# First attention: the maximum and the exponential of wide score tiles in two pieces

## The reference

```python
scores = jnp.einsum('bqd,bkd->bqk', Qr, Kr) / jnp.sqrt(jnp.float32(d))
mask = jnp.tril(jnp.ones((T, T), dtype=bool), k=1)
scores = jnp.where(mask[None, :, :], scores, -jnp.inf)
attn = jax.nn.softmax(scores, axis=-1)
out = jnp.einsum('bqk,bkd->bqd', attn, V)
```

## Time and profile before

| | before |
|---|---|
| median of 3 runs | 703.73 us |
| lowest to highest | 703.64 to 704.94 us |
| profiled execution | 704.66 us |
| its span | 702.9 us |
| granted TensorE clock | 0.994 |
| TensorE busy in the span | 634.1 us, 90% |
| VectorE busy | 528.9 us, 75% |
| ScalarE busy | 489.2 us, 70% |
| GpSimd busy | 188.3 us, 27% |

### The profile page before, as it was taken

How to read it: one execution, slowest core, us unless ns; L and a number is a source line. 1 busy time by engine, 2 the same in 40 slices (tenths; PEclk the granted TensorE clock), 3 DMA queues, 4 the chain that set the end, 5 groups by cost and what they waited for, 6 DMA issues and landing times.

```text
span 702.9 us, 9405 instructions
## 1 busy us (share of the span) xinstructions
PE 634.1 (90%) x3324; PEld 272.4 (39%) x3324; DVE 528.9 (75%) x993; ACT 489.2 (70%) x503; POOL 188.3 (27%) x250
## 2 busy tenths in 40 slices
PE   7989899999999899889988888898898788899996
PEld 4677345464464423223222112122231111266555
DVE  6876512427155399999899999999999999676775
ACT  4656324225333499999999999999999989444431
POOL 4532240212102041491148101705600006022012
PEclk9999999999999999999999999999999989999999
DMA  5430200002204301234013510111102103300171
GB/s 171 134 137 1 92 1 0 2 0 59 77 1 137 111 11 47 57 105 138 5 57 97 151 56 11 49 57 56 31 27 57 56 3 120 119 1 1 41 232 30
DMA packets 33230, 44.60 MB, mean 63 GB/s; under 512 B 5408, under 2 KB 20000, under 8 KB 32800
## 3 DMA queue, kind: packets, MB, share of 16 engines
q1 hardware_dynamic: 33184, 44.01, 21.1%
HBM read 31.60 MB, written 10.55 MB: 60 GB/s over the span
## 4 chain that ended last, share of the span: by engine, by line
PE 43%; ACT 23%; DVE 21%; issue 11%; POOL 1%; DVEq 0%; ACTq 0%
ACT w_hh L1138 19%; PE ps L778 8%; PE ps L788 8%; DVE hid L1482 5%; DVE hid L1477 5%; PE ps L813 5%; PE ps L760 4%; PE ps L690 3%; PE ps L671 3%; PE ps L744 2%; PE ps L822 2%; ACT probs L1109 2%; DVE st L1240 2%; PE ps L587 1%; PE ps L493 1%
## 5 line engine op out<-in xcount | busy, mean ns | idle before, releaser
L1138 ACT ACTIVATE w_hh<-hid 128x2048 f32<-128x2048 f32 x128 | 249.9, 1952 | 8.3 <-DVE hid L1482 7.8
L690 PE MATMUL ps<-w_hh,v_h 128*32 128x512 f32 x1024 | 137.8, 610 | 33.4 <-ACT w_hh L1138 32.3
L1477 DVE TENSOR_TENSOR hid<-ps,probs 128x1024 f32<-128x1024 f32 x86 | 104.5, 1215 | 19.4 <-ACT probs L1109 16.1
L671 PE MATMUL ps<-q_s,k_s 64*128 64x512 bf16 x256 | 99.3, 389 | 14.7 <-DVE hid L1477 14.1
L1482 DVE SCALAR_TENSOR_TENSOR hid<-ps,probs 128x1024 f32<-128x1024 f32 x86 | 104.7, 1217 | 4.6 <-PE ps L671 3.3
L671 PE MATMUL ps<-q_w,k_w 64*128 64x512 bf16 x256 | 99.4, 389 | 0.0
L1109 ACT ACTIVATE probs<-ps 128x1024 f32<-128x1024 f32 x86 | 91.3, 1062 | 2.2 <-PE ps L671 2.2
L671 PE MATMUL ps<-q_g,k_s 128*128 128x512 bf16 x256 | 78.3, 388 | 1.1 <-ACT qkv_a L1109 1.1
L671 PEld LDWEIGHTS ps<-q_w,k_w 64*128 64x128 bf16 x256 | 23.7, 92 | 107.2 <-issue 55.3
L788 PE MATMUL ps<-hid,w_hh 128*128 128x512 f32 x128 | 56.3, 592 | 0.0
L778 PE MATMUL ps<-hid,w_hh 128*128 128x512 f32 x128 | 55.8, 594 | 0.0
(11 more groups left out here) (314 smaller groups left out, 1001.2 us busy)
## 6 DMA issues: line engine op xcount, KB each, us to landing
qk_rows<-part SPq DMA_DIRECT2D x48, 128.0 KB, 2.4
w_hh<-w_rows SPq DMA_DIRECT2D x4, 1024.0 KB, 8.8
qk_rows<-part_g SPq DMA_DIRECT2D x24, 128.0 KB, 2.4
q_g<-qk_rows SPq DMA_DIRECT2D x32, 96.0 KB, 2.2
k_s<-qk_rows SPq DMA_DIRECT2D x32, 96.0 KB, 2.3
q_s<-qk_rows SPq DMA_DIRECT2D x32, 96.0 KB, 2.4
k_w<-qk_rows SPq DMA_DIRECT2D x32, 96.0 KB, 2.5
q_w<-qk_rows SPq DMA_DIRECT2D x32, 96.0 KB, 2.4
```

Source lines behind the costliest of these rows:

```text
L671: last = mm(ps[:, base + half, :], k_op[rows, u, keys], q_op[rows, u, half * CHUNK:(half + 1) * CHUNK], start=True, stop=True)
L690: last = mm(ps[VW * g4:VW * g4 + VW, 6, :], v_h[:, u, mt, :], ee[:, mt % 2, g4 * CHUNK:(g4 + 1) * CHUNK], start=(mt == 0), stop=(mt == BT ...
L1138: A(ee[:, mt % 2, :], zz[:, mt % 2, :], ACT.Exp).then_inc(S["e"], 1)
L1477: v.tensor_tensor(zz[:, mt % 2, 0:SEQ], banks[:, 2 * CHUNK:4 * CHUNK], gg[s % 3], ALU.add).then_inc(S["z1"], 1)
```

## The change

For tiles with i >= 4 the maximum and the exponential are each made in two pieces, columns 0 to 511 and the rest; tiles with i < 4 keep one piece. `a_scores` counts `s_a` after each bank, so the first maximum waits for the first bank alone. `nmx` is now made from both maxima, the second one read as an operand per row. Each exponential has a sum of its own, `rsum` and `rsum_1`, and `a_next` adds them before the reciprocal. `a_turn` waits for the first exponential before its first four transposes and for the second before the fifth. The counts of `e_a` and `s_a` are kept by `pieces_to`. The order of the tiles and of the other work on each engine stays as it was.

```diff
--- before.py
+++ after.py
@@ -204,6 +204,7 @@
         sm = sb("sm", [P, SM_W])
         tiny = sb("tiny", [P, 64])
         nlam = sb("nlam", [P, 1])
+        mx_1, rsum_1 = tiny[:, 0:TILES], tiny[:, TILES:2 * TILES]
         cs_tab = sb("cs_tab", [P, 2, CT, HEADS, 2])
         raw = sb("raw", [P, 2, CHUNK])
         sq = sb("sq", [P, 2, CHUNK])
@@ -325,6 +326,13 @@
             if b == 0 and i < 2:
                 return 1
             return 2 * b + (2 if P * (i + 1) < CHUNK else 3)
+
+        def pieces(t):
+
+            return 2 if t % BT >= CT else 1
+
+        def pieces_to(t):
+            return sum(pieces(u) for u in range(t + 1))
 
         def att_width(i):
 
@@ -548,7 +556,7 @@
                 pe.wait_ge(S["ropeq"], seen)
                 pe.wait_ge(S["ropek"], seen)
                 if t >= 2:
-                    pe.wait_ge(S["e_a"], t - 1)
+                    pe.wait_ge(S["e_a"], pieces_to(t - 2))
                 w = att_width(i)
                 for n0 in range(0, w, CHUNK):
                     n1 = min(w, n0 + CHUNK)
@@ -560,17 +568,21 @@
                     if masked:
                         last = mm(ps[:, bank, m0 - n0:m1 - n0], ident_bf[:],
                                   mask[:, m0 - P * i:m1 - P * i], start=False, stop=True)
+                    if n0 == 0 and pieces(t) == 2:
+                        last.then_inc(S["s_a"], 1)
                 last.then_inc(S["s_a"], 1)
 
             def a_turn(t):
                 i = t % BT
-                pe.wait_ge(S["e_a"], t + 1)
+                pe.wait_ge(S["e_a"], pieces_to(t) - pieces(t) + 1)
                 if t == 0:
                     pe.wait_ge(S["vout"], 2)
                 if t == 4:
                     pe.wait_ge(S["vout"], CHUNKS)
                 pe.wait_ge(S["pe_a"], t)
                 for j in range(i + 1):
+                    if j == CT:
+                        pe.wait_ge(S["e_a"], pieces_to(t))
                     last = nc.tensor.transpose(ps[:, 4 + j // CT, (j % CT) * P:(j % CT + 1) * P],
                                                probs[:, t % 2, j * P:(j + 1) * P], ident[:])
                 last.then_inc(S["pt_a"], 1)
@@ -989,8 +1001,10 @@
                 if t >= 2:
                     act.wait_ge(S["pt_a"], t - 1)
                 base = 2 * CHUNK * (t % 2)
-                A(probs[:, t % 2, 0:w], banks[:, base:base + w], ACT.Exp, bias=nmx[:, t:t + 1],
-                  scale=ATT_SCALE, accum_out=rsum[:, t:t + 1]).then_inc(S["e_a"], 1)
+                for i, total in enumerate((rsum, rsum_1)[0:pieces(t)]):
+                    n0, n1 = i * CHUNK, w if i == pieces(t) - 1 else CHUNK
+                    A(probs[:, t % 2, n0:n1], banks[:, base + n0:base + n1], ACT.Exp, bias=nmx[:, t:t + 1],
+                      scale=ATT_SCALE, accum_out=total[:, t:t + 1]).then_inc(S["e_a"], 1)
 
             def a_turned(t):
                 i = t % BT
@@ -1317,10 +1331,18 @@
 
             def a_max(t):
                 w = att_width(t % BT)
-                dve.wait_ge(S["s_a"], t + 1)
                 base = 2 * CHUNK * (t % 2)
-                me.step(v.tensor_reduce(mx[:, t:t + 1], banks[:, base:base + w], AX.X, ALU.max))
-                v.tensor_scalar(nmx[:, t:t + 1], mx[:, t:t + 1], -ATT_SCALE, None, ALU.mult).then_inc(S["m_a"], 1)
+                if pieces(t) == 2:
+                    dve.wait_ge(S["s_a"], pieces_to(t) - 1)
+                    me.mark(v.tensor_reduce(mx_1[:, t:t + 1], banks[:, base:base + CHUNK], AX.X, ALU.max))
+                n0 = CHUNK * (pieces(t) - 1)
+                dve.wait_ge(S["s_a"], pieces_to(t))
+                me.step(v.tensor_reduce(mx[:, t:t + 1], banks[:, base + n0:base + w], AX.X, ALU.max))
+                if pieces(t) == 2:
+                    v.tensor_scalar(nmx[:, t:t + 1], mx[:, t:t + 1], mx_1[:, t:t + 1], -ATT_SCALE,
+                                    ALU.max, ALU.mult).then_inc(S["m_a"], 1)
+                else:
+                    v.tensor_scalar(nmx[:, t:t + 1], mx[:, t:t + 1], -ATT_SCALE, None, ALU.mult).then_inc(S["m_a"], 1)
 
             def a_add(c):
                 dve.wait_ge(S["yn_a"], c + 1)
@@ -1328,10 +1350,12 @@
 
             def a_next(t):
 
-                dve.wait_ge(S["e_a"], t + 1)
+                dve.wait_ge(S["e_a"], pieces_to(t))
                 w = P * (t % BT + 1)
                 if t % BT < BT - 1:
                     me.mark(v.tensor_copy(p_next[:, t:t + 1], probs[:, t % 2, w:w + 1]))
+                if pieces(t) == 2:
+                    me.step(v.tensor_tensor(rsum[:, t:t + 1], rsum[:, t:t + 1], rsum_1[:, t:t + 1], ALU.add))
                 me.step(v.reciprocal(rinv[:, t:t + 1], rsum[:, t:t + 1]))
 
             def a_post(t):
```

## The result

| | before | after |
|---|---|---|
| median of 8 runs | 703.93 us | 706.50 us |
| lowest to highest | 703.43 to 704.98 | 705.85 to 708.75 |
| profiled execution | 704.66 us | 707.50 us |
| its span | 702.9 us | 705.7 us |

The ratio after to before is 1.0040, 95% interval 1.0027 to 1.0054: slower by 1.9 to 3.8 us. The forecast had the sign right and the size wrong: 705.3 us, +1.57, against +2.6 between the medians. (The forecast added to a median of 703.73 us from three executions; the median of eight is 703.93.)

A forecast was written before the change was run, and what follows sets the result against it. VectorE was taken to bound the kernel up to tile 7, then TensorE with ScalarE close behind, VectorE again before tile 15. Terms 1.03 + 0.54 = +1.57 us on a median of 703.73 gave 705.3 us; range 704.1 to 706.4.

The forecast's parts named there:

- The bound: First attention: VectorE's order of work sets exponential starts up to tile 7 (41.06 us); then TensorE, with ScalarE close behind.
- Part 1, second maximum: Maximum of each wide tile on VectorE: the second piece adds 0.08 us (bounds 0.06 and 0.16), earning nothing.
- part 2, pointer: `nmx` of each wide tile, reading the second maximum through a pointer: +0.07 us (bounds 0 and 0.10).
- Part 3, the addition: Adding the two sums on VectorE between copy and reciprocal: 0.17 us each (bounds 0.13 and 0.22).
- rival B: Expensive operations at tiles 7 and 15: no overlap (0.16), addition 0.22, pointer 0.10; 2.3 us, 706.0 us; chance 0.17.
- Part 4 and the sum: Two-piece exponential: ScalarE free 0.24 us later, transposes end 0.23 sooner; all terms: 1.03 (batch one) + 0.54 (tile 15) = +1.57.
- The slack of 0.15 us: ScalarE's margin before TensorE loads tile 8's transpose; subtracted from the 1.18 us shift, leaving 1.03.
- The two rules weighed beside the rows: Skill rules: next operation waits for an empty pipe (sum 1.97, 705.7 us); small tiles pay fixed latency (0.158 and 0.244).
- C: Hand-over by halves works: each wide tile's chain 0.6 us shorter, 4.9 us on eight tiles; 698.8 us; chance 0.05.
- A: Same mechanism, cheap operations at tiles 7 and 15: pointer free, addition 0.13; 1.1 us, 704.8 us; chance 0.28.
- its rider: Addition to rival B: `nmx` of tile 5 or 6 also stands behind GpSimd (0.93 us); 706.6 us.
- D: Pieces start no earlier and VectorE's additions are absorbed by stalls; only ScalarE's 0.24 us stays; 704.0 us; chance 0.05.

The follow-up runs named there:

- e1: The changed kernel with the addition of the two sums written as a tensor_scalar through a pointer; stage +1.61 us against the kernel before, ratio 1.0021.
- e4: The changed kernel with the exponential in one piece again (no second sum, no addition), maximum in two; stage +0.73 us against the kernel before, ratio 1.0010.
- e6: The kernel before with GpSimd's four rotary additions cut from 512 columns to 8 each; stage -0.98 us against the kernel before, ratio 0.9981.
- e2: The kernel before plus one 128x1 tensor_tensor ahead of the reciprocal of each wide tile; stage +1.62 us against the kernel before, ratio 1.0022.

## Why the prediction was wrong

*The bound.* Right. VectorE set the time up to tile 7, and every 0.1 us put on it there appeared in the stage (e1 to e4). TensorE is close behind, though: with GpSimd's additions cut it sets part of the time (e6), which the prediction did not say.

*Part 1, second maximum, and part 2, pointer.* Right. The pieces start 0.61 us apart, 0.08 short of the first one's 0.69, and `nmx` took 0.214 us instead of 0.153. All eight second maxima start 0.60 to 0.61 us after the first. Priced 0.15 a tile; taking the split of the maximum away gave 0.66 for five tiles, 0.13 each.

*Part 3, the addition.* This step failed. I took 0.17 us, between a step of another stage (0.15) and the step behind the reciprocal of tile 4 (0.18), and gave 0.22 as the upper bound. At tile 4 it took 1.17 us, 1.0 more than priced, and it lay on the path: without it (e1) the stage is 0.86 us shorter, although the addition through the pointer takes 0.05 us more than the free one each time. The signs were in front of me. I had used the post-scaling held up by GpSimd and let only `nmx` stand behind GpSimd as an addition to rival B, for 0.6 us. I did not ask the same of the addition, although it runs at 36.2 us, while GpSimd works until 37.4, and although the rows that I used show no `tensor_tensor` on two SBUF tensors beside GpSimd. I also halved the merged row of GpSimd's two operations and so read the post-scaling as ending 0.3 us behind the first; that one ends at 36.16 (34.50 + 1.66), and the scaling 0.08 us later, at 36.24: it waits for the end of the first and the addition for the end of the second. A bound from below or above has to come from a row in the same neighbourhood, not only of the same size. The Trainium skill says it too ("SBUF — State Buffer", section "SBUF: two separate sides"): a VectorE instruction in a mode with two ports, or one with two SBUF inputs when the GpSimd instruction reads SBUF, and the GpSimd instruction exclude each other; whichever starts first keeps the other out until it is done. The runs agree (1.17 to 1.19 us until GpSimd's end, three kinds; GpSimd's 1.66 instead of 1.27 behind VectorE), and I had not weighed it.

*Part 4 and the sum.* Right. Without the hold-up, the exponential of tile 7 in e1 was 0.97 us late against tile 4's maximum (0.94 forecast), the stage +1.61 (1.57). The way through ScalarE's norm behind tile 7 and tile 15 was as forecast: from tile 7 to tile 11 the shift in the changed kernel grew from 1.89 to 1.98 us, which is 0.24 - 0.15, and the tail added 0.49 (0.54 forecast; 0.55 in e1). The transposes of tile 15 ended 2.15 us after the start of the exponential (2.12 forecast) instead of 2.35, and that was useless, as said.

*The slack of 0.15 us.* I took it off the whole shift. It belongs only to the way through ScalarE; e2 and e4, with one-piece exponentials, kept the whole shift of tile 7.

*The two rules weighed beside the rows.* The Trainium skill's section "The DRAIN you can't avoid" ("VectorE: DVE Perf Modes") adds that a next operation that is not held starts earlier; the prediction left that out. Here the second maxima start 0.08 us before the end of the first, so the extra 0.4 us of that paragraph did not come. The section on the errata speaks of operations that read SBUF, while the 0.158 and 0.244 us are from operations that read PSUM: these rows do not bear it out.

*The rivals.* C (the hand-over by halves, 0.05) did not come: one wide maximum in eight would have waited for scores, and the changed kernel has no wait for TensorE ahead of a wide maximum. A and B had the right mechanism at other prices. B's sum of 2.3 us comes near the measured 2.47, and its rider's 706.6 near the median of 706.5, but by luck: operations do overlap, and what is held up is the addition, while all eight `nmx` took 0.21 us. D did not hold.

*The range* ended at 706.4, the median was 706.5; that this is so near is due to B's terms in the range, not to the forecast, which missed by 0.9 us in the stage. The upper end left the hold-up out; with 1.0 us for it on top of B's 706.0, it would have reached 707.

## What to carry to other kernels

Before a small VectorE operation is priced from a row elsewhere, look at what GpSimd does at the same moment: on one column per partition 0.15 us became 1.2 because of two SBUF operands, and the same sum through a pointer took 0.20. Splitting an operation paid here only where its consumer is the one that waits and no further work stands behind it on the split engine; the fixed parts (0.08 and 0.07 us a maximum, 0.24 an exponential) are paid on each of eight wide tiles, part of them on the path, and the split earned 0.2 us in one place, in the trace. Once the chain of waits shows which queue sets the time, moving unrelated work from ahead of the critical instruction to behind it was worth more than the split (0.88 us of stage against 0.19).

## What the runs showed of the hardware that I had not expected

Beside a GpSimd `tensor_tensor` on SBUF (512 columns, 1.27 us when nothing holds it), a VectorE instruction that starts second waited for the end of the GpSimd instruction if it had two SBUF operands, even of one column (`tensor_tensor` 1.17 us, `scalar_tensor_tensor` 1.18), or copied four columns (1.19) or scaled 128 (0.92) of one. A copy of one column (0.14), an addition to one column through a pointer (0.20), a reduction from PSUM (1.09 for 897 columns) and a `scalar_tensor_tensor` with one operand in PSUM (0.34) did not wait. Whether two or three columns wait was not tried. GpSimd waits in its turn when VectorE is first (1.66 us instead of 1.27). So these two engines, of which the opening says that they meet only at semaphores, here also held each other up without one.

In the run with addition and reciprocal ahead of the last scaling the granted clock was 0.79 and 0.78 in the two stretches of 4 us behind the stage, and eight products took 5.37 us instead of 3.67. This was seen in one profiled execution; what brought it about was not tested.
